# Computing the first norm's two modulation blocks as rows and transposing them, with the set-up loads and small tables in another order

## The reference

```python
mod = (_silu(L0_c) @ L0_wmod).reshape(L0_c.shape[0], 6, 1, -1)
sa, ca, ga, sb, cb, gb = (mod[:, 0], mod[:, 1], mod[:, 2], mod[:, 3], mod[:, 4], mod[:, 5])
...
h = _layernorm(x, axis=-1) * (1 + ca) + sa
x = x + ga * _L0_attn_ref(h, Wq, Wk, Wv, Wo, bank_weights, memories, memory_norms)
h = _layernorm(x, axis=-1) * (1 + cb) + sb
x = x + gb * _L0_ffn_ref(h, w_gate, w_up, w_down)
```

## Time and profile before

| | us |
|---|---|
| median of 3 executions | 1457.63 |
| lowest, highest | 1454.31, 1458.93 |
| the profiled execution, its own time | 1454.72 |
| its span, first to last instruction | 1452.9 |
| PE busy in the span | 1397.4 (96%) |
| DVE, POOL, ACT busy | 901.7, 552.4, 510.4 |
| mean granted TensorE clock | 0.988 |

### The profile page before, as it was taken

The page is one execution under the profiler, slowest core; times in us unless marked ns, Lnnn a source line. Parts: engine busy times, 40 slices in busy tenths (PEclk is TensorE's granted clock), DMA queues, the critical chain, the costliest instruction groups (busy, mean ns, idle before and its releaser), DMA issues.

```text
span 1452.9 us, 18904 instructions
## 1 busy us (share of the span) xinstructions
PE 1397.4 (96%) x6890; PEld 1155.1 (80%) x6890; DVE 901.7 (62%) x1287; ACT 510.4 (35%) x794; POOL 552.4 (38%) x363
## 2 busy tenths in 40 slices
PE   8999999998989999999999999999999999999997
PEld 7577887777768888888888887878888888888885
DVE  5778888887666556364555557494645555563644
ACT  5455665555732222222222223332222222222221
POOL 0756666665234323231313335462313133232311
PEclk9999999999999999999999999999999999999999
DMA  7202122113330102020211213130202111020102
GB/s 261 96 30 104 70 87 87 61 54 117 127 142 29 66 29 94 0 94 0 94 48 46 94 39 113 58 152 1 95 0 94 41 53 65 29 94 0 65 0 94
DMA packets 24040, 102.41 MB, mean 70 GB/s; under 512 B 3012, under 2 KB 3524, under 8 KB 14284
## 3 DMA queue, kind: packets, MB, share of 16 engines
q1 hardware_dynamic: 24012, 102.05, 18.8%
HBM read 68.47 MB, written 33.57 MB: 70 GB/s over the span
## 4 chain that ended last, share of the span: by engine, by line
PE 79%; DVE 12%; issue 4%; ACT 2%; DMA 1%; POOL 1%; DVEq 0%; POOLq 0%; ACTq 0%; SPq 0%
PE bank L1074 25%; PE bank L1076 24%; PE bank L1075 24%; DVE banks_r L904 2%; PE bank L1102 2%; DVE h_abs L1026 1%; PE bank L1152 1%; DVE x_ring L869 1%; PE bank L1085 1%; DVE one_each L1014 1%; PE bank L1093 1%; PE bank L1162 1%; DVE pair_lo L1008 1%; DVE combT_lo L875 1%; DVE inv_norm L894 1%
## 5 line engine op out<-in xcount | busy, mean ns | idle before, releaser
L989 DVE TENSOR_TENSOR h_act<-bank,silu_g 128x512 f32<-128x512 f32 x128 | 88.0, 690 | 404.7 <-PE bank L1076 384.0
L446 POOL TENSOR_TENSOR hs_lo<-h_abs,hs_hi 128x512 fp32r<-128x512 f32 x128 | 174.9, 1396 | 417.5 <-ACT hs_hi L663 417.5
L402 POOL TENSOR_TENSOR h_lo<-h_raw,h_hi 128x512 fp32r<-128x512 f32 x64 | 125.1, 1984 | 236.7 <-ACT h_hi L646 236.7
L1074 PE MATMUL bank<-h_hi,up_w_hi 128*128 128x512 f32 x512 | 201.1, 393 | 7.2 <-DVE h_act L989 6.0
L1074 PE MATMUL bank<-h_hi,gate_w_hi 128*128 128x512 f32 x512 | 200.1, 391 | 6.0 <-ACT silu_g L669 3.2
L1074 PE MATMUL bank<-down_w_hi,hs_hi 128*128 128x512 f32 x512 | 199.6, 390 | 2.9 <-POOL hs_lo L446 2.9
L1075 PE MATMUL bank<-h_lo,up_w_hi 128*128 128x512 f32 x512 | 200.3, 391 | 0.0
L1076 PE MATMUL bank<-h_hi,up_w_lo 128*128 128x512 f32 x512 | 200.2, 391 | 0.0
L1076 PE MATMUL bank<-h_hi,gate_w_lo 128*128 128x512 f32 x512 | 199.5, 390 | 0.0
L1075 PE MATMUL bank<-h_lo,gate_w_hi 128*128 128x512 f32 x512 | 199.3, 389 | 0.0
L1076 PE MATMUL bank<-down_w_hi,hs_lo 128*128 128x512 f32 x512 | 199.2, 389 | 0.0
(11 more groups left out here) (131 smaller groups left out, 2446.8 us busy)
## 6 DMA issues: line engine op xcount, KB each, us to landing
h_raw<-h2T_scratch SPq DMA_DIRECT2D x16, 1024.0 KB, 4.8
x_ring<-in_x_dram SPq DMA_DIRECT2D x8, 1024.0 KB, 4.8
x_scratch<-x_ring SPq DMA_DIRECT2D x8, 1024.0 KB, 3.9
h2T_scratch<-h_full SPq DMA_DIRECT2D x8, 1024.0 KB, 3.9
over_x<-x_scratch SPq DMA_DIRECT2D x8, 1024.0 KB, 4.8
acc_scratch<-over_x SPq DMA_DIRECT2D x8, 1024.0 KB, 3.9
over_x<-acc_scratch SPq DMA_DIRECT2D x8, 1024.0 KB, 4.8
out_dram<-over_x SPq DMA_DIRECT2D x8, 1024.0 KB, 3.9
```

The source lines that it names most:

```text
L402: nc.gpsimd.tensor_tensor(h2_lo[:, k], h2_raw[:, k], h2_hi[:, k].bitcast(F32), ALU.subtract).then_inc(h2_lo_done, 1)
L446: nc.gpsimd.tensor_tensor(hs_lo[:, j], h_abs[:, j], hs_hi[:, j].bitcast(F32), ALU.subtract).then_inc(hs_lo_done, 1)
L989: nc.vector.tensor_tensor(h_act[:, cc, j], bank[2 * (j % 2) + 1][:], silu_g[:, j % 2], ALU.mult).then_inc(h_done, 1)
L1074: nc.tensor.matmul(out_, stat[0], mov[0], start=start, stop=False)
```

## The change

Blocks SA and CA are computed by `mod_row`, as the other four, into banks 4 and 5: 4 rows of 512 each. ACT copies each row block into SBUF (`first_row(0)` ahead of `ln_sqrt`, `first_row(1)` behind the normalization), in the tile `gates` under the name `first_rows`. PE transposes the 8 pieces of 4x128 into bank 3 (`row_columns`), between `t1(0, 1)` and `t1(0, 2)`, and DVE takes the mods from there. The tables and loads are put in another order: SP issues wq ahead of norm_raw, and bank_sb ahead of mem_raw; DVE does wq_lo and the mods ahead of the bank_sb steps, and mem_bd behind `h1_low(0)`; ACT does mem_hi behind the first `sigma_exp`, and so behind the Exp of bank_sb; PE does the `active_mm` matmul behind `q_block(0, 0)`; the load of GB waits for row SA only. The counts that later waits use go up by two.

```diff
@@ -125,6 +125,7 @@
             mod_rows = gate_sign
+            first_rows = gates
             ln_raw = sba("ln_raw", [P, 2, S, 6])
@@ -252,15 +253,15 @@
                 load_mod(CA, wmod_sb[:, 1])
-                sp.dma_start(norm_raw[:], norm_hd.rearrange("(k p) n -> p k n", p=P)).then_inc(norm_in, 16)
-                sp.dma_start(mem_raw[:], mem_hd.rearrange("(k p) n e -> p k n e", p=P)).then_inc(norm_in, 16)
-                sp.dma_start(bank_sb[:], bank_w.partition_broadcast(P)).then_inc(norm_in, 16)
                 sp.dma_start(banks_r[0][:].rearrange("p a b c -> p a (b c)"),
                              wqT.rearrange("(k p) n -> p k n", p=P)).then_inc(wq_in, 16)
+                sp.dma_start(norm_raw[:], norm_hd.rearrange("(k p) n -> p k n", p=P)).then_inc(norm_in, 16)
+                sp.dma_start(bank_sb[:], bank_w.partition_broadcast(P)).then_inc(norm_in, 16)
+                sp.dma_start(mem_raw[:], mem_hd.rearrange("(k p) n e -> p k n e", p=P)).then_inc(norm_in, 16)
                 load_mod(GA, x_ring[:, place(2)])
...
                 sp.dma_start(x_ring[:, place(1)], x_t[1]).then_inc(x_in[place(1)], 16)
-                sp.wait_ge(mods_mm, 1)
+                sp.wait_ge(rows_mm, 1)
                 load_mod(GB, wmod_sb[:, 0])
@@ -563,18 +564,27 @@
+            def first_row(i):
+                act.wait_ge(rows_mm, i + 1)
+                nc.scalar.activation(first_rows[:, i], bank[4 + i][0:B, :], ACT.Copy).then_inc(rows_done, 1)
+            first_row(0)
             ln_sqrt(0, 0)
             normalize(0, 0, xn1, xn1_done)
+            first_row(1)
             act.wait_ge(wq_in, 16)
...
             h1_split(0, first=True)
-            act.wait_ge(mem_bd_ready, 1)
-            nc.scalar.activation(mem_hi[:], xn2[:, :, 0:NB * HALF], ACT.Copy).then_inc(wa_hi, 1)
             act.wait_ge(bank_shifted, 1)
             nc.scalar.activation(bank_sb[:], bank_sb[:], ACT.Exp).then_inc(bank_exp, 1)
-            sigma_all(0, first=True)
+            def memories():
+                act.wait_ge(mem_bd_ready, 1)
+                nc.scalar.activation(mem_hi[:], xn2[:, :, 0:NB * HALF], ACT.Copy).then_inc(wa_hi, 1)
+            sigma_all(0, first=True, between=memories)
             act.wait_ge(wo_in, 16)
@@ -585,7 +595,7 @@
                 act.wait_ge(gates_ready, 1)
-                act.wait_ge(rows_mm, i + 1)
+                act.wait_ge(rows_mm, i + 3)
                 nc.scalar.activation(mod_rows[:, i], bank[7][0:B, :], ACT.Copy).then_inc(rows_done, 1)
@@ -800,12 +810,20 @@
             ln_scalars(0, 0)
+            dve.wait_ge(wa_hi, 1)
+            nc.vector.tensor_tensor(wq_lo[:], banks_r[0][:].rearrange("p a b c -> p a (b c)"),
+                                    wq_hi[:].bitcast(F32), ALU.subtract)
+            dve.wait_ge(mods_mm, 1)
+            mm, mm2 = (bank[i][:, 0:2 * K * B].rearrange("p (i k b) -> p i k b", i=2, k=K) for i in (3, 6))
+            nc.vector.tensor_copy(mods[:, 0], mm[:, 0])
+            nc.vector.tensor_scalar(mods[:, 1], mm[:, 1], 1.0, None, ALU.add).then_inc(mods_ready, 1)
             dve.wait_ge(norm_in, 48)
             link(nc.vector.tensor_reduce(bank_red[:], bank_sb[:], AX_X, ALU.max))
...
                                     ALU.subtract).then_inc(bank_shifted, 1)
+            h1_low(0)
@@ -817,15 +835,6 @@
             ins.then_inc(mem_bd_ready, 1)
-            dve.wait_ge(wa_hi, 1)
-            nc.vector.tensor_tensor(wq_lo[:], banks_r[0][:].rearrange("p a b c -> p a (b c)"),
-                                    wq_hi[:].bitcast(F32), ALU.subtract)
-            dve.wait_ge(mods_mm, 1)
-            mm, mm2 = (bank[i][:, 0:2 * K * B].rearrange("p (i k b) -> p i k b", i=2, k=K) for i in (7, 6))
-            nc.vector.tensor_copy(mods[:, 0], mm[:, 0])
-            nc.vector.tensor_scalar(mods[:, 1], mm[:, 1], 1.0, None, ALU.add).then_inc(mods_ready, 1)
-            h1_low(0)
@@ -1076,16 +1085,6 @@
-            def mod_scalars(i, block_):
-                pe.wait_ge(wmod_in[block_], 16)
-                for f in range(K):
-                    for k in range(K):
-                        at = (i * K + f) * B
-                        ins = nc.tensor.matmul(bank[7][:, at:at + B], wmod_sb[:, i, k, f * P:(f + 1) * P],
-                                               silu_c[:, k], start=(k == 0), stop=(k == K - 1))
-                return ins
             def mod_row(block_, staged, to):
@@ -1094,8 +1093,8 @@
             pe.wait_ge(silu_c_ready, 1)
-            mod_scalars(0, SA)
-            mod_scalars(1, CA).then_inc(mods_mm, 1)
+            mod_row(SA, wmod_sb[:, 0], bank[4]).then_inc(rows_mm, 1)
+            mod_row(CA, wmod_sb[:, 1], bank[5]).then_inc(rows_mm, 1)
@@ -1173,18 +1172,28 @@
+            def row_columns(src, to):
+                for i in range(2):
+                    for f in range(K):
+                        at = (i * K + f) * B
+                        ins = nc.tensor.transpose(to[:, at:at + B], src[:, i, f * P:(f + 1) * P], ident[0:B, 0:B])
+                return ins
             pe.wait_ge(ident_ready, 1)
-            for k in range(K):
-                if k == 1:
-                    pe.wait_ge(mods_ready, 1)
-                t1(0, k)
+            t1(0, 0)
+            t1(0, 1)
+            pe.wait_ge(rows_done, 2)
+            row_columns(first_rows, bank[3]).then_inc(mods_mm, 1)
+            t1(0, 2)
+            t1(0, 3)
+            pe.wait_ge(wa_hi, 1)
+            q_block(0, 0, first=True)
             pe.wait_ge(consts_ready, 1)
...
                              start=True, stop=True).then_inc(active_mm, 1)
-            pe.wait_ge(wa_hi, 1)
-            for g in range(K):
+            for g in range(1, K):
                 q_block(0, g, first=True)
@@ -1218,7 +1227,7 @@
                     if first:
-                        pe.wait_ge(rows_done, 1)
+                        pe.wait_ge(rows_done, 3)
                     t1(t + 1, 1)
@@ -1253,14 +1262,9 @@
-                    pe.wait_ge(rows_done, 2)
+                    pe.wait_ge(rows_done, 4)
                     pe.wait_ge(clip_done, 4)
-                    for i in range(2):
-                        for f in range(K):
-                            at = (i * K + f) * B
-                            ins = nc.tensor.transpose(bank[6][:, at:at + B], mod_rows[:, i, f * P:(f + 1) * P],
-                                                      ident[0:B, 0:B])
-                    ins.then_inc(mods_mm, 1)
+                    row_columns(mod_rows, bank[6]).then_inc(mods_mm, 1)
                 else:
```

## The result

| | us, median (lowest to highest) | executions |
|---|---|---|
| before | 1454.32 (1451.70 to 1458.93) | 20 |
| changed | 1458.06 (1456.05 to 1462.13) | 20 |

Ratio of changed to before 1.0025, 95% interval 1.0016 to 1.0034: slower by 3.7 us (2.3 to 4.9). The median is inside the range of 1455.5 to 1462.5, and 0.25% is inside the 0.3%, though the interval reaches past it. The sum was +1.8, half of what was measured; the absolute figure of 1459.4 came near 1458.06 in part because it stood on a median of three executions that was 3.3 us too high.

The account below looks back on a forecast made before the run. The prediction saw the set-up bound by two nearly equal paths, L1085's small matmuls and x tile 0 through Sqrt to wq_lo; +1.55 and +0.24 made +1.8 us on 1457.63, so 1459.4, range 1455.5 to 1462.5.

Parts of the forecast that it names:

- the 0.3%: Whole kernel: about 4.4 us, what a measurement of this kernel can tell from no change.
- The sum: Set-up: +1.55 at the first h1_full and +0.24 for L1184 make +1.8 us.
- the absolute figure: Whole kernel: 1459.4 us, from the median 1457.63 of the shown runs plus 1.8.
- Part 1: PE's rows replacing L1085: row SA ends at 12.55, clock rising after 4.4 us; row CA ends at 16.0.
- Part 2: ACT: first row copy (0.59) and table load (1.28) ahead of Sqrt, which starts at 14.5 instead of 12.31.
- Part 3: From Sqrt through normalization, wq_hi, wq_lo and mods: first h1_full at 23.15 against 21.58, +1.55.
- Part 4: From h1_full to q blocks: same work, plus L1184 now between the first two q blocks, +0.24 (0 to 0.5).
- Part 5: Memories moved behind h1_low(0): mem_lo to 35.2 against 32.6, costing nothing, with over 4 us of cover.
- I let the shift go through in full: Behind the set-up: rows GA, GB and all that follows hang on q's end, so the whole +1.8 us reaches the time.
- either way: Rival, phase A: the shift changes when the clock falls later, moving the time some us; chance 0.07.
- The removed time: Rival, set-up: 13.8 us of matmuls become 6.9 at full clock and the gain is won, 1450.7; chance 0.03.
- stay low over both rows: Rival, PE's rows SA and CA: ending at 13.8 and 20.7, in sum +5.7, 1463.3; chance 0.10.

Follow-up runs that it names:

- the first trace: The changed kernel's first trace against the one trace of before: DVE's read of row GB at 45.12 against 43.80, span 1458.6 against 1452.9.
- the plain delay: The kernel before with the last four small matmuls of block CA done twice, against the kernel before: median 1456.23, ratio 1.0013.
- the first interval: The changed kernel against the kernel before, 20 executions each: median 1458.06, ratio 1.0025, interval 1.0016 to 1.0034.
- the second: The changed kernel timed again against the kernel before, beside the delayed kernel: median 1457.61, ratio 1.0020, interval 1.0006 to 1.0034.
- the kernel with the rows alone: Rows, copies and transposes with loads, DVE steps, mem_hi and active_mm in the old order, against the kernel before: 1457.79, ratio 1.0012.

## Why the prediction was right, and where it was off

- **Part 1, the rows.** Row SA's end: 12.55 forecast, 12.43 measured; landing, steps and clock rise as read from the earlier trace rows. Row CA was done at 15.85 (16.0).
- **Part 2, copy and table load.** The deciding term, and right: copy, load, Sqrt at 14.35 (14.5). Load and Sqrt follow each other within 0.01, so the 1.38 us of drain that the Trainium skill (ScalarE: Activation LUTs, What ACT_TABLE_LOAD costs) adds to a switch isn't seen here; its rule on the place of the load (Step-by-step: what each stage is for) held in all kernels.
- **Part 3.** First h1_full +1.15 instead of +1.55. Sqrt was 0.15 earlier than forecast, and ACT starts an operation about 0.1 before the last one's end (17.83 against 15.00 + 2.92), twice on this path, where I had added full durations; the rest is rounding. The mods ended 0.17 behind wq_lo, as forecast. The small transposes took 0.65 at 2.4 GHz, and 1.01 in the two traces with the clock at 1.2 there; they were hidden in all.
- **Part 4.** L1194 came between the first two q blocks; with it and the start of the second block the shift went from 1.1 (29.56 against 28.44, where L1194 and before's second block start) to 1.3 (29.70 against 28.44). L1194's term is 0.14 where I had put 0.24.
- **Part 5.** The memories stayed hidden: row GB waited for nothing but row GA.
- **The sum** for the set-up: +1.8 forecast, +1.3 in the first trace, +0.8 to +1.8 in four.
- **The absolute figure** was luck in part. The base, 1457.63, was the median of three executions and lay 3.3 us above the 1454.32 of twenty; the shift was put 1.9 us too low; the two errors partly cancel. The change itself, +3.7, lies above the +0.8 to +3.5 that the prediction gave it, though its interval (2.3 to 4.9) reaches into that.
- **The mis-sized step** is "I let the shift go through in full". For the plain delay nothing contradicts it (+1.7 at the mark, +1.6 in the median, interval 0 to 3.6). Every other kernel's interval also holds what its mark gives. Those of the changed kernel lie high: +1.3 gives 1.0009, below the first interval, which begins at 1.0016; +0.8 gives 1.0006, the very edge of the second. So in the first comparison at least 1 us, by the medians 2.4, is lost behind the set-up, or at least 0.5 with the highest of the four marks. The traces place it where TensorE falls to 1.2 GHz, and two of the four have none of it. I had that as a rival "either way" at 0.07, with no other price than "some us". Why the changed kernel should meet more of these falls is open, and with one trace of before even their number is compared only through the mean clock. That its set-up ends when the clock lets it, and so no longer at random against the clock's changes, is an argument, not shown; the kernel with the rows alone is tied to the clock in the same way, and its interval (1.0002 to 1.0023) holds the 1.0013 of its mark.
- **Rivals.** The removed time (13.79 - 9.15) was not won; the clock did not stay low over both rows.

## What to carry to other kernels

Before an engine's operation is moved ahead of another on ScalarE, look which table the later one needs: a copy in front of it takes the table load out of the idle time and puts it on the path. Making the longest group of a set-up shorter gives nothing while a second path of the same length runs beside it; here the gain came when the copies went to the idle engine and the mods ahead of a 2.3 us subtraction, by the rows mostly from the second. And where a gap lets TensorE's clock fall in some executions and not in others, one trace against one trace says little: compare marks ahead of the gaps, and the times over many executions.

## What the runs showed of the hardware that I had not expected

- A fall of TensorE's clock in one tile costs about 1.6 us, and it may be made up in another tile in which the other kernel has its fall; the times of one kernel on one chip spread over 6 to 7.5 us, for which such falls are the likely reason, though no run here separates them from others.
- With PE at work on four matmuls on constants from 1.07 to 7.19 us, the next row took 3.60 us, instead of 5.73 in the changed kernel.
